# A two-stage fp32 kernel: sums and pair products of the mixing stage in a new order, feed-forward turns by VectorE and a DRAM round trip

## The reference

```
x = x + xattn(ctx, ctx, layernorm(x))    # x, ctx: 16 x 512 x 1024; 64 heads of 8 rows
  kv  = einsum('bhil,bhjl->bijhl', k, v)      # k = v = ctx, so kv is symmetric in i and j
  y   = causal convolution of kv with ssm_kernel[h] along l, + kv * D[h]
  out = einsum('bijhl,bhil->bjhl', y, q)      # q = layernorm(x)
x = x + moe(layernorm(x))                # 8192 tokens of width 1024
  scores = sigmoid(x @ router_w); 8 of 32 experts a token (best 4 of 8 groups, then top 8)
  routed = sum over the picks of  w * (silu(x @ w_gate[e]) * (x @ w_up[e])) @ w_down[e]
  shared = silu(x @ sw_gate) * (x @ sw_up) @ sw_down
```

## Time and profile before

| | us |
|---|---|
| median of 3 runs | 15187.83 |
| lowest, highest | 15181.02, 15187.87 |
| the profiled execution's own time | 15246.89 |
| its span, first to last instruction | 15245.2 |

### The profile page before, as it was taken

The page is one execution under the profiler, slowest core; times in us unless marked ns, Lnnn a source line. Parts: engine busy times, 40 slices in busy tenths (PEclk is TensorE's granted clock), DMA queues, the critical chain, the costliest instruction groups (busy, mean ns, idle before and its releaser), DMA issues.

```text
span 15245.2 us, 197610 instructions
## 1 busy us (share of the span) xinstructions
PE 14289.3 (94%) x67488; PEld 11857.7 (78%) x67489; DVE 5359.1 (35%) x5312; ACT 3085.2 (20%) x4072; POOL 4221.1 (28%) x4357
## 2 busy tenths in 40 slices
PE   7777777769999999999999999999999999999999
PEld 6666666558888888888888888788888888888887
DVE  6656666631221222212212122323112112545544
ACT  3323333211111112211212122312111111111111
POOL 5556666521111111111111111111111111333333
PEclk9888888879999999999999999999999999999999
DMA  3454434331221222212212222423112111665666
GB/s 100 82 82 81 83 82 82 67 74 58 74 76 58 75 75 106 92 58 75 97 68 78 72 90 92 148 74 107 71 59 75 58 60 50 210 208 199 209 208 200
DMA packets 482743, 1491.05 MB, mean 98 GB/s; under 512 B 87745, under 2 KB 87873, under 8 KB 482450
## 3 DMA queue, kind: packets, MB, share of 16 engines
q0 software_dynamic: 286720, 890.00, 17.4%
q1 hardware_dynamic: 177938, 531.68, 13.7%
q10 hardware_dynamic: 17920, 67.12, 1.1%
HBM read 1083.97 MB, written 421.38 MB: 99 GB/s over the span
## 4 chain that ended last, share of the span: by engine, by line
PE 78%; DMA 0%; DVE 0%; issue 0%; ACT 0%; DVEq 0%; ACTq 0%; SPq 0%; POOLq 0%; POOL 0%
PE gps L1255 24%; PE ups L1255 24%; PE yps L1255 24%; PE xps L1262 4%; PE hps L1295 2%; DVE wlo L1183 0%; DMA raw<-in_L_ffn_w_up_dram 0%; ACT whi L1121 0%; DMA xg<-xnd,idx 0%; DVE yrow L1209 0%; DMA picked<-yd,gidx 0%; ACTq L1003 0%; DVEq L1003 0%; DVE xlo L1183 0%; DVE hlo L1183 0%
## 5 line engine op out<-in xcount | busy, mean ns | idle before, releaser
L1100 POOL DMA_INDIRECT yd<-yrow,yidx x544 | 575.8, 1058 | 7815.1 <-DVE yrow L1233 7815.1
L1219 DVE TENSOR_TENSOR hb<-hb,ups 128x512 f32<-128x512 f32 x672 | 461.8, 687 | 6190.9 <-ACT hb L1140 6190.9
L1255 PE MATMUL gps<-whi,xhi 128*128 128x512 f32 x5376 | 2156.0, 401 | 34.5 <-DVE wlo L1183 30.9
L1255 PE MATMUL ups<-whi,xlo 128*128 128x512 f32 x5376 | 2115.6, 394 | 0.0
L1255 PE MATMUL gps<-wlo,xhi 128*128 128x512 f32 x5376 | 2113.9, 393 | 0.0
L1255 PE MATMUL ups<-whi,xhi 128*128 128x512 f32 x5376 | 2110.8, 393 | 0.0
L1255 PE MATMUL gps<-whi,xlo 128*128 128x512 f32 x5376 | 2110.6, 393 | 0.0
L1255 PE MATMUL ups<-wlo,xhi 128*128 128x512 f32 x5376 | 2092.6, 389 | 0.0
L1140 ACT ACTIVATE hb<-gps 128x512 f32<-128x512 f32 x672 | 402.5, 599 | 6727.3 <-PE ups L1255 6717.1
L1255 PE MATMUL yps<-whi,hhi 128*128 128x512 f32 x5376 | 1726.7, 402 | 4.5 <-DVE hlo L1183 4.5
L1255 PE MATMUL yps<-wlo,hhi 128*128 128x512 f32 x5376 | 1674.7, 393 | 0.0
(11 more groups left out here) (165 smaller groups left out, 18316.3 us busy)
## 6 DMA issues: line engine op xcount, KB each, us to landing
raw<-in_L_ffn_w_gate_dram SPq DMA_DIRECT2D x128, 512.0 KB
raw<-in_L_ffn_w_up_dram SPq DMA_DIRECT2D x128, 512.0 KB
raw<-in_L_ffn_w_down_dram SPq DMA_DIRECT2D x64, 1024.0 KB
kT<-in_ctx_dram SPq DMA_DIRECT2D x64, 704.0 KB, 10.7
xin<-in_x_dram SPq DMA_DIRECT2D x64, 512.0 KB
thi<-kph SPq DMA_DIRECT2D x64, 512.0 KB, 6.8
tlo<-kpl SPq DMA_DIRECT2D x64, 512.0 KB, 8.4
xres<-in_x_dram SPq DMA_DIRECT2D x64, 512.0 KB
```

The costliest lines, as they stand in the source:

```text
L1100: pool.indirect_dma_start(out=yd, in_=yrow[i][:, :], in_offset=None, out_offset=bass.IndirectOffsetOnAxis(ap=yidx[i][:, 0:1], axis=0), bou ...
L1219: dve.tensor_tensor(hb[:, :], hb[:, :], ups[:, :], ALU.mult).then_inc(h_done, 1)
L1255: ins = pe.matmul(ps, rows, w[:, chunk, i * 512:(i + 1) * 512], start=first and n == 0, stop=last_one and n == 2)
```

## The change

Mixing stage. `prod` becomes two tiles for two time blocks each, of 5 rows of pairs instead of 8 terms: the two products of a pair lie side by side, so that a sum reads 5 times 2 adjacent elements (one half row is a zero that is written once). Opposite pairs and sum are one call for each of the four groups (`opposite_and_sum`), and they come one group later than the products. `xin` is two buffers and its load is the first of SP's step. The transposes for routing come ahead of those of the output on PE, the logits ahead of the last group. Routing on DVE is cut into four parts in steps 4 to 7, the list DMAs are in steps 0 to 6 of the block after (the sixth and seventh tile together in step 6), and 32 of them instead of 16 stand behind the last step.

Feed-forward. The 12 transposes of a tile leave PE. The rows are gathered as quarters by four indirect DMAs of 128 pieces of 1 KB; DVE turns 32 x 32 blocks (`x_turn`) into the PSUM tile `xt`. The product h goes to a PSUM tile, DVE turns its blocks into `hb`, ACT issues four DMAs that write it to DRAM (`spread_h`, pieces of 512 B) and one that reads it back in the order that PE wants (`collect_h`), and waits for it ahead of the high part of h. ACT takes x of the next tile ahead of silu. Picks are added after the result of the matmuls and after the low part of h, and the row is stored when all four are added. Weights lie in DRAM in the order of the blocks, gate and up in one tensor, loaded by one DMA for each unit where there were two.

The core of the diff:

```diff
-        prod = sb("prod", [P, LB // 2, HD * HD * B])
+        prod = [sb(f"prod{i}", [P, 2, SLOTS]) for i in range(2)]
...
             def step(s):
+                if s.on(NORM):
+                    n, i = s.n(NORM), s.slot(NORM)
+                    wait(sp, xin_mm, n - 1)
+                    sp.dma_start(xin[i][:, :], head_rows(x, n)).then_inc(x_ld[i], 16)
...
-                dve.wait_ge(y_used, GROUPS * n + g + 1)
...
+                dve.wait_ge(y4_used, GROUPS * n + g + 1)
                 wait(dve, out_mm, n - 1)
-                dve.tensor_reduce(osb[s.slot(k)][:, 4 * h:4 * h + 4, :],
-                                  prod[:, :, :].rearrange("p m (t c) -> p m c t", t=HD), AXX, ALU.add)\
-                    .then_inc(reduced, 1)
-                dve.wait_ge(reduced, 2 * n + h + 1)
+                dve.tensor_reduce(osb[s.slot(k)][:, 2 * g:2 * g + 2, :],
+                                  view(to, 0, 0, [[SLOTS, 2], [2, P], [PLANE, ROWS], [1, 2]]),
+                                  mybir.AxisListType.XY, ALU.add).then_inc(reduced, 1)
+                dve.wait_ge(reduced, GROUPS * n + g + 1)
...
             def step(s):
                 times_queries(s, TAIL, 3)
-                reduce(s, TAIL, 1)
-                if routes(s, 4, 1):
-                    choose(s.block - 1)
-                if routes(s, 5, 1):
+                opposite_and_sum(s, TAIL, 2)
+                times_queries(s, CONV, 0)
+                opposite_and_sum(s, TAIL, 3)
+                if routes(s, 6, 1):
                     count(s.block - 1)
-                times_queries(s, CONV, 0)
                 times_queries(s, CONV, 1)
                 if s.on(NORM):
                     dve.wait_ge(sqrt_in, s.n(NORM) + 1)
                     wait(dve, normed, s.n(NORM))
                     scale_and_shift(sd_in, mv_in).then_inc(scale_in, 1)
-                opposite_pairs(s, CONV, 0)
-                reduce(s, CONV, 0)
+                opposite_and_sum(s, CONV, 0)
+                if routes(s, 4, 1):
+                    choose_groups(s.block - 1)
+                if routes(s, 5, 1):
+                    choose(s.block - 1)
+                if routes(s, 7, 1):
+                    assign(s.block - 1)
+                times_queries(s, CONV, 2)
                 if s.on(OUT):
                     n, xr = s.n(OUT), xres
                     dve.wait_ge(r_ld, 16 * (n + 1))
                     dve.wait_ge(out_mm, n + 1)
                     dve.tensor_tensor(xr[:, :], xr[:, :], ps[:, :], ALU.add).then_inc(out_added, 1)
-                if routes(s, 5, 1):
-                    assign(s.block - 1)
-                times_queries(s, CONV, 2)
+                opposite_and_sum(s, CONV, 1)
                 if s.on(OUT):
                     dve.wait_ge(sqrt_out, n + 1)
                     wait(dve, normed2, n)
                     scale_and_shift(sd_out, mv_out).then_inc(scale_out, 1)
-                opposite_pairs(s, CONV, 1)
...
+                if s.on(OUT):
+                    pe.wait_ge(reduced, GROUPS * (s.n(OUT) + 1))
+                    wait(pe, q_copied, s.past(INS) + int(s.on(INS)))
+                    wait(pe, x2T_copied, s.past(ROUTE) + int(s.on(ROUTE)))
+                    for m in range(LB):
+                        last = pe.transpose(ps[:, m * P:(m + 1) * P], osb[s.slot(OUT)][:, m, :], ident)
+                    last.then_inc(out_mm, 1)
...
             def gather(t, slot, turns):
-                wait(pool, xT_mm, t - 1 if not isinstance(t, int) else max(t - 1, 0))
+                wait(pool, x_turned, t - 1 if not isinstance(t, int) else max(t - 1, 0))
                 pool.wait_ge(idx_ld[slot], 16 * (turns + 1))
-                settle(pool, pool_turns)
-                pool.indirect_dma_start(out=xg[slot][:, :], out_offset=None, in_=xnd,
-                                        in_offset=bass.IndirectOffsetOnAxis(ap=idx[slot][:, 0:1], axis=0))\
-                    .then_inc(x_ld[slot], 16)
+                pool.tensor_tensor(xidx[slot][:, :], idx[slot][:, :], quad[:, :], ALU.add).then_inc(xidx_ready, 1)
+                pool.wait_ge(xidx_ready, t + 1)
+                for q in range(QUADS):
+                    settle(pool, pool_turns)
+                    pool.indirect_dma_start(out=xg[slot][:, q, :], out_offset=None, in_=quarters,
+                                            in_offset=bass.IndirectOffsetOnAxis(ap=xidx[slot][:, q:q + 1], axis=0))\
+                        .then_inc(x_ld[slot], 16)
...
+                act.wait_ge(x_turned, t + 1)
+                wait(act, gu_mm, t)
+                act.activation(xhi[:, :, :], xt[:, :, :], ACT.Copy).then_inc(x_hi, 1)
+            def spread_h(t, slot):
+                act.wait_ge(h_turned, t + 1)
+                for q in range(QUADS):
+                    act.dma_start(hsd[slot].rearrange("(b r) q x -> r b q x", r=SQ)[:, :, q, :],
+                                  hb[q * SQ:(q + 1) * SQ, :].rearrange("r (b x) -> r b x", x=P)).then_inc(h_st, 16)
+            def collect_h(t, slot):
+                act.wait_ge(h_st, 16 * QUADS * (t + 1))
+                wait(act, h_lo, t)
+                act.dma_start(hz[:, :, :, :].rearrange("p q k s -> p (q k s)"),
+                              hsd[slot].rearrange("p q x -> p (q x)")).then_inc(h_ld, 16)
...
-                act.wait_ge(y_dve, c.n(-1))
+                act.wait_ge(pick_used, K // 2 * (c.n(-2 - SH0) + 1))
...
+            def x_turn(t, slot, turns):
+                dve.wait_ge(x_ld[slot], 16 * QUADS * (turns + 1))
+                wait(dve, x_lo, t)
+                dve.transpose(xt[:, :, :].rearrange("p k t -> p (k t)"),
+                              xg[slot][:, :, :].rearrange("p q (k r) -> p k q r", r=SQ)).then_inc(x_turned, 1)
...
+                    dve.tensor_tensor(hp[:, :], hb[:, :], ups[:, :], ALU.mult).then_inc(h_done, 1)
+                    dve.wait_ge(h_done, t + 1)
+                    dve.transpose(hb[:, :], hp[:, :]).then_inc(h_turned, 1)
...
+                if c.part(-1) is not None:
+                    dve.wait_ge(y_dve, t)
+                    add_picks(c.n(-1 - SH0), i, c.half(-1 - SH0), c.part(-1))
...
-                if c.on(1):
-                    transpose_rows(c.n(1), c.slot(1), c.half(1))
...
-                if c.on():
-                    pe.wait_ge(h_done, t + 1)
-                    for m in range(KH):
-                        last = pe.transpose(hps[:, m * P:(m + 1) * P], hb[:, m * P:(m + 1) * P], ident)
-                    last.then_inc(hT_mm, 1)
```

More of the change, by code:

```diff
@@ L57 @@
 UNITS = GU + DN
+SQ = 32
+QUADS = P // SQ
+KX, KH = L // P, I // P
 C_ID, C_TRI, C_ONE = 0, 128, 256
@@ L1257, in three @@
                 return ins
-            def transpose_rows(t, slot, turns):
-                pe.wait_ge(x_ld[slot], 16 * (turns + 1))
-                for m in range(KX):
-                    last = pe.transpose(xps[:, m * P:(m + 1) * P], xg[slot][:, m * P:(m + 1) * P], ident)
-                last.then_inc(xT_mm, 1)
             def tile(c):
```

271 lines of the change are left out of this document (146 added, 125 removed).

## The result

The changed kernel takes 14,807.8 us (median of 4 runs, 14,792.7 to 14,816.7), before 15,184.4 on the same chip: ratio 0.9751, interval 0.9734 to 0.9768. The forecast was 14,230 with a range of 13,780 to 14,650: the direction was right, the time lies 578 us above the forecast and outside the range. The profiled execution takes 14,806.9 us, 440 us less than that of before.

A forecast was written before the change was run, and what follows sets the result against it. PE was taken to bound the feed-forward, no engine the mixing stage, where PE waits for the residual. -713 + 66 + 205 - 540 + 21 (ends) = -961 from 15246.9, less 59, gave 14,230 us, range 13,780 to 14,650.

The forecast's parts named there:

- Mixing stage, -540: Mixing stage: no residual wait, faster sums and early x cut steps from 47.6 to 38 us, 56 steps x 9.6.
- the 59 us that the prediction takes off at the end: Whole kernel: the profiled execution before was 59 us above the runs' median, so 14,286 became 14,227.
- Routed tiles, -713: Routed feed-forward tiles: 1.31 us of transposes leave PE in each of 544 tiles, the replacement hidden beside the matmuls.
- Changes of expert, +66: Routed feed-forward, 33 new experts: h comes some 2 us after PE wants it, adding 66 us.
- 5.6 us for four high parts of 1.9 us: At a new expert ACT makes four weight high parts before issuing h's write, so h comes 5.6 us later, at 18.7.
- the slowest rival: Feed-forward: the round trip bounds every tile, making the kernel slower than before; 16,010 us at legs of 12, chance 0.05.
- Shared tiles, +205: Shared feed-forward tiles: a loop without PE takes 19.4 us instead of 17.8, over 128 tiles.
- The loop: Shared tiles: store issue, x, silu, product, turn, h round trip, low part, four picks, back to the store; 19.4 us.
- 1.5 + 6.5: Shared tiles' h trip: 1.5 us for three issues, 6.5 for the legs, write to DRAM and read back, 3.2 each.
- the rival of 10 us: Feed-forward: both legs take 10 us, shared tiles +650, experts +180, total 14,790 us; chance 0.10.
- The page's rule: h round trip: 2.0 us fixed plus bytes over 436 GB/s, legs 2.15 and 2.6 us; not used in the sum.
- The rule on lines of 16 bytes: Mixing-stage sums: two consecutive accesses to one 16-byte line suffice for full bandwidth, so pairs run at 2.86 us.

The follow-up runs named there:

- e5b: Changed kernel with 56 unused floats (224 bytes) a partition ahead of `xhi`; 14,627 us, ratio 0.9614 to the kernel before.
- e11: Changed kernel with 104 unused floats (416 bytes) a partition ahead of `xhi`; ratio 0.9648 to the kernel before.
- e12: Kernel before the change with 80 unused floats (320 bytes) ahead of `xhi`; ratio 0.9968, 48 us faster than without them.
- e6b: Changed kernel loading only an eighth of each weight piece from the second expert on, output not the reference's; ratio 0.9691 to the kernel before.
- e2: Changed kernel with a shared tile's four picks added ahead of the matmul result and the low part of h; 14,272 us, ratio 0.9380 to before.
- e4: Changed kernel whose mixing-stage sums add elements 512 bytes apart, output not the reference's; ratio 0.9874 to the kernel before.

## Why the prediction was wrong

- **Mixing stage, -540: the mechanism right, the size met with luck.** Shown as said: sums of 2.86 (2.82), the residual's wait gone, clock 0.96. But the step is 39.5 us where 38 was said: from the ninth head to the last the mean falls from 47.6 to 39.4 us, which is 55 x 8.2 = 451 us and not 540. The other 90 of the 541 are 42 us in the first eight steps, which the sum left out, and 46 behind the last head's x, nearly all of it the one long step of the profiled execution of before. That step is also in the 59 us that the prediction takes off at the end: on the median the stage gains some 480, not 525 with its ends. The prediction passed over x in a sentence, as one of two waits. The runs make it a condition: without the second buffer some 320 of the gain are lost, because the new order puts a copy that PE needs behind the wait for x.
- **Routed tiles, -713: the time of what stays was taken as fixed.** "Without these 1.31 us it is 16.51 us" subtracts the transposes and keeps the matmuls' 0.229. They take 0.2333, 72 x 0.0044 = 0.32 us more a tile; the median tile is 16.86 us, 0.35 above 16.51, and 544 x 0.35 = 190 us are missing. e5b, e11 and e12 show that the cause is where the operands lie in the partition, by all that was tried the distance between stationary and moving ones, which the new tensors ahead of `xhi` shifted. No row of before shows it; the kernel's list of tensors does.
- **Changes of expert, +66: too small and put to the wrong wait.** The excess over 16.86 us a tile is 171 us, 37 before. A simple one costs 1.6 us, but PE waits there for the first low part of the weights, which on ACT and DVE comes behind x, silu, product and turn; PE waits for h seven times only, 9.7 us in all. The prediction also counts 5.6 us for four high parts of 1.9 us, which make 7.6, and gives no reason for the difference. The rest comes from experts with one tile, where h's write waits behind 6 MB (e6b). The prediction had that competition only as "for it" of the slowest rival.
- **Shared tiles, +205: right mechanism, the trip too short.** The loop was named with all its members. The mean tile is 21.57 us where 19.4 was said, and 128 x 2.17 = 278 us. 1.9 of the 2.2 us are the trip: 9.9 us from first issue to use for 1.5 + 6.5. Of these the issues have their share (three take 1.9 us in the mean, for 1.5), the legs are 8.0 us in the mean for 6.5. The forecast's 3.2 us a leg came from loads that ran almost alone, here write, picks and store meet. At 8.0 the legs lie between the forecast and the rival of 10 us, whose 6.6 us store was the nearer row for this stage. Mean traffic does not explain them, since e2 has shorter trips at 248 GB/s. In the routed tiles the legs take 4.0 us in the median.
- **The page's rule** for a DMA issued by POOL, 2.0 us and bytes over 436 GB/s (the Trainium skill, *DMA: Bandwidth & Descriptors*, Anatomy of one DMA), would have had 4.75 for both legs, by the prediction's estimate. These DMAs are issued by ACT; the estimate is near the 4.3 of the routed tile shown and far under the 9.05 of the shared one.
- The rule on lines of 16 bytes (the Trainium skill, *SBUF — State Buffer*, Door 1: The DMA port swizzle) agrees with e4: 1.10 ns per element in pairs, 1.87 apart.

The three misses are 190 us for the matmuls, 68 at changes of expert (171 - 37 - 66) and 278 in the shared tiles with the last one's picks, 536 in all. The other 40 or so are the mixing stage's, 525 forecast and some 480 on the median: some 580, the whole of the error.

## What to carry to other kernels

When work leaves the bound engine, look for loops that the rest of the change closes without it, and look at what else the loop starts just ahead of their transfers; loads that ran alone were too cheap a price, and the mean traffic of the stage is none either. Here moving four additions from one side of a wait to the other was worth some 590 us. A tensor added ahead of others moves their addresses: compare the distance between a matmul's stationary and moving operand before and after, and try a pad where the spacing of matmuls is longer than elsewhere. Compare stages as well as totals: a hold in one execution or on one chip can stand for a gain in the sum. A buffer and an order can need each other, so undo them one at a time and add them one at a time.
